# A macaron block on one core: the sums of two of eight batches in the second scoring pass made by accumulating transfers

## The reference

```
x = x + 0.5 * routed_ffn(layernorm(x))     # first pass of the router
x = x + attention(layernorm(x))
x = x + 0.5 * routed_ffn(layernorm(x))     # second pass of the router
```

## Time and profile before

| | us |
|---|---|
| median of 3 runs | 4295.17 (4293.64 to 4295.38) |
| the profiled execution itself | 4294.03 |
| its span in the profile | 4292.0 |
| second scoring pass, first issue of SP to first instruction of the token choice | 3816.65 to 3932.39 |

### The profile page before, as it was taken

The page is one execution under the profiler, slowest core; times in us unless marked ns, Lnnn a source line. Parts: engine busy times, 40 slices in busy tenths (PEclk is TensorE's granted clock), DMA queues, the critical chain, the costliest instruction groups (busy, mean ns, idle before and its releaser), DMA issues. The chain is left out here.

```text
span 4292.0 us, 59690 instructions
## 1 busy us (share of the span) xinstructions
PE 3592.8 (84%) x20178; PEld 1422.3 (33%) x20178; DVE 3187.8 (74%) x4122; ACT 3242.9 (76%) x6717; POOL 2988.4 (70%) x1166
## 2 busy tenths in 40 slices
PE   0376784699999999999999999999999999930376
PEld 0243452233333333333333333333333333310243
DVE  8644674888888888888888888888888888628544
ACT  3544673589988898998898899899889989834433
POOL 2011001399999999999999999999999989975211
PEclk9988897799999999999999999999999999965598
DMA  6500899589999999999999999999999999888300
GB/s 210 168 5 3 296 391 313 118 180 194 210 198 204 206 199 205 198 212 198 204 207 197 207 196 209 202 202 208 198 207 200 206 202 195 170 214 277 124 5 5
DMA packets 335683, 809.46 MB, mean 189 GB/s; under 512 B 27596, under 2 KB 211424, under 8 KB 271648
## 3 DMA queue, kind: packets, MB, share of 16 engines
q0 software_dynamic: 66432, 475.04, 54.9%
q1 hardware_dynamic: 223008, 284.46, 22.7%
q10 hardware_dynamic: 45952, 46.27, 3.1%
HBM read 198.90 MB, written 136.48 MB: 78 GB/s over the span
## 5 line engine op out<-in xcount | busy, mean ns | idle before, releaser
L1703 ACT ACTIVATE at_probs<-at_ps_s 128x512 f32<-128x512 f32 x4096 | 2261.9, 615 | 256.4 <-PE at_ps_s L1813 248.9
L1562 POOL TENSOR_TENSOR at_pool_sum<-at_pool_sum,at_probs 128x2048 f32<-128x2048 f32 x448 | 2173.6, 4852 | 27.8 <-DMA at_probs<-at_probs 20.0
L1592 DVE TENSOR_REDUCE at_part_max<-at_ps_max 128x3 f32<-128x1536 f32 x1024 | 1801.0, 1759 | 428.6 <-PE at_ps_max L1736 428.3
L1813 PE MATMUL at_ps_s<-at_qs,at_ks 97*128 97x512 f32 (+1 forms) x4096 | 1524.4, 451 | 6.4 <-ACT at_probs L1703 5.1
L1782 PE MATMUL at_ps_acc<-at_probs,at_v 128*32 128x512 f32 x8192 | 1092.7, 605 | 0.9 <-ACT at_probs L1703 0.9
L1813 PEld LDWEIGHTS at_ps_s<-at_qs,at_ks 97*128 97x128 f32 (+1 forms) x4096 | 626.5, 188 | 1103.5 <-ACT at_probs L1703 815.5
L1594 DVE TENSOR_REDUCE at_part_max<-at_max_copy 128x1 f32<-128x512 f32 x1024 | 691.7, 675 | 0.0
L1655 ACT COPY at_max_copy<-at_ps_max 128x512 f32<-128x512 f32 x1024 | 610.0, 596 | 102.2 <-PE at_ps_max L1736 102.0
L1541 POOL DMA_DIRECT2D at_probs<-at_probs x448 | 399.7, 892 | 288.4 <-ACT at_probs L1703 240.1
L1736 PE MATMUL at_ps_max<-at_ks,at_qs 32*128 32x512 f32 x4096 | 525.5, 500 | 83.0 <-DMA at_ks<-qk_parts 49.3
L1736 PEld LDWEIGHTS at_ps_max<-at_ks,at_qs 32*128 32x128 f32 x4096 | 197.8, 183 | 442.2 <-issue 393.4
(11 more groups left out here) (196 smaller groups left out, 2405.0 us busy)
## 6 DMA issues: line engine op xcount, KB each, us to landing
at_probs<-at_probs POOLq DMA_DIRECT2D x448, 1024.0 KB, 8.3
qk_parts<-pr_hi SPq DMA_DIRECT2D x32, 1024.0 KB, 12.1
qk_parts<-pr_lo SPq DMA_DIRECT2D x32, 1024.0 KB, 12.3
at_qs<-qk_parts SPq DMA_DIRECT2D x320, 64.0 KB, 5.5
at_ks<-qk_parts SPq DMA_DIRECT2D x80, 256.0 KB, 5.2
rows_tile<-in_x SPq DMA_DIRECT2D x16, 1024.0 KB, 11.9
after_ffn<-rows_tile ACTq DMA_DIRECT2D x16, 1024.0 KB
v_tokens<-pr_v SPq DMA_DIRECT2D x32, 512.0 KB, 10.9
```

The source lines that it names most:

```text
L1562: nc.gpsimd.tensor_tensor(acc, first, probs[:, slot(unit, c)], ALU.add).then_inc(pool_added, 1)
L1592: nc.vector.reduce_max(part_max[:, 0:HG - 1, t, c], ps_max[:, 0:HG - 1], AX.X).then_inc(three_max_done, 1)
L1703: nc.scalar.activation(probs[:, slot(unit, c), h], ps_s[:, BANK[unit, j]], ACT.Exp, scale=SCALE).then_inc(exp_done, 1)
L1813: nc.tensor.matmul(ps_s[:, BANK[unit, j]], ks[rows, g, h, c * P:(c + 1) * P], qs[rows, unit % NQB, h, :], start=True, stop=True).then_inc( ...
```

## The change

Batches 3 and 7 are taken out of the pieces; 24 pieces are left (`PARTS`). For each of the two, SP issues one load of 2 MB of residual rows into `rows.tile` (L177 of the changed kernel) behind the last piece of the batch three before, and GpSimd, once that has landed and after the last piece of the batch two before is added, issues one accumulating transfer of 2 MB (L220) that reads `attention` from memory and adds it onto the held rows. VectorE and the products of GpSimd in these two batches wait for that transfer's semaphore (`dma_summed`) in place of `added`. The products keep their tiles and their number, 32; those of a batch made by transfer follow in one row. Nothing else in the program is changed.

```
+    DMA_BATCHES = (3, 7) if adding else ()
+    PARTS = [(b, p) for b in range(B) if b not in DMA_BATCHES for p in range(PIECES)]
...
+                b, p = PARTS[n]
+                first = b * S + p * PIECE * P
+                tiles = slice(p * PIECE, (p + 1) * PIECE)
                 if n >= NADD:
 
                     sp.wait_ge(added, n - NADD + 1)
...
-                for n in range(1, B * PIECES):
+                for n in range(1, len(PARTS)):
                     load_both(n)
+                    for b in DMA_BATCHES:
+                        if PARTS[n] == (b - 3, PIECES - 1):
+                            sp.dma_start(rows.tile[:, b], x[b * S:(b + 1) * S, :].rearrange("(t p) d -> p t d", p=P)
+                                         ).then_inc(dma_x_in[b], 16)
...
-                if adding:
-                    pool.wait_ge(added, n + 1)
+                if b in DMA_BATCHES:
+                    pool.wait_ge(dma_summed[b], 16)
+                elif adding:
+                    pool.wait_ge(added, PARTS.index((b, n % PIECES)) + 1)
...
-                    if n >= 1:
-                        product(n - 1)
-                product(B * PIECES - 1)
+                    while done < b * PIECES + p:
+                        product(done)
+                        done += 1
+                    if p == PIECES - 1 and b + 2 in DMA_BATCHES:
+                        pool.wait_ge(dma_x_in[b + 2], 16)
+                        nc.gpsimd.dma_start(rows.tile[:, b + 2], add[(b + 2) * S:(b + 3) * S, :]
+                                            .rearrange("(t p) d -> p t d", p=P), accum_op=ALU.add
+                                            ).then_inc(dma_summed[b + 2], 16)
+                while done < SHARED:
+                    product(done)
+                    done += 1
...
-                    if adding and t % PIECE == 0:
-                        dve.wait_ge(added, b * PIECES + t // PIECE + 1)
+                    if b in DMA_BATCHES and t == 0:
+                        dve.wait_ge(dma_summed[b], 16)
+                    elif b not in DMA_BATCHES and adding and t % PIECE == 0:
+                        dve.wait_ge(added, PARTS.index((b, t // PIECE)) + 1)
```

More of the change, by code:

```diff
@@ L123, in score_rows @@
         added = sem("added")
+        dma_x_in = {b: sem(f"dma_x_in{b}") for b in DMA_BATCHES}
+        dma_summed = {b: sem(f"dma_summed{b}") for b in DMA_BATCHES}
         own_done = sem("own")
@@ L150, in load_both @@
                 k = n % NADD
-                first = n * PIECE * P
-                tiles = slice(n % PIECES * PIECE, (n % PIECES + 1) * PIECE)
+                b, p = PARTS[n]
+                first = b * S + p * PIECE * P
+                tiles = slice(p * PIECE, (p + 1) * PIECE)
                 if n >= NADD:
                     sp.wait_ge(added, n - NADD + 1)
-                sp.dma_start(rows.tile[:, n // PIECES, tiles],
+                sp.dma_start(rows.tile[:, b, tiles],
                              x[first:first + PIECE * P, :].rearrange("(t p) d -> p t d", p=P)).then_inc(both_in[k], 16)
@@ L194, in _ @@
             if adding:
-                for n in range(B * PIECES):
-                    tiles = slice(n % PIECES * PIECE, (n % PIECES + 1) * PIECE)
+                done = 0
+                for n, (b, p) in enumerate(PARTS):
+                    tiles = slice(p * PIECE, (p + 1) * PIECE)
                     pool.wait_ge(both_in[n % NADD], n // NADD * 32 + 32)
-                    nc.gpsimd.tensor_tensor(rows.tile[:, n // PIECES, tiles], rows.tile[:, n // PIECES, tiles],
+                    nc.gpsimd.tensor_tensor(rows.tile[:, b, tiles], rows.tile[:, b, tiles],
                                             addend[:, n % NADD], ALU.add).then_inc(added, 1)
```

## The result

The changed kernel takes 4306.87 us (median of 8 runs, 4304.01 to 4312.37), the kernel before 4294.74 (8 runs, 4290.31 to 4298.59): a ratio of 1.003, 95% interval 1.0019 to 1.0041, or 8 to 18 us more. It is slower. The other half is no merit or fault of the forecast: the median grew by 12.1 us, 3 less than the pass of the profiled execution did, which is within the scatter of the stages around it.

The account below looks back on a forecast made before the run. The DMA engines at 348 GB/s were taken as the bound. Last landing 3926.8 plus 2.3 + 2.4 + 9.7 gives 3941.2 against 3922.95, +18.2; 4294.03 + 18.2 = 4312.2, forecast 4313 against the median, range 4299 to 4327 us.

Parts of the forecast that it names:

- The bound: Second scoring pass: the DMA engines set the pace, 348 GB/s for 1 KB rows; GpSimd's relief is worth little.
- the estimate by the Trainium skill's 425 GB/s: Second scoring pass: with loads at 425 GB/s, DMA engines' sum 90 us and the change about 6 us faster; not adopted.
- The cost of a transfer: Each 2.10 MB accumulating transfer: 81 ns per 1 KB run and engine, 10.4 us, against 47 ns and 6.0 us plain.
- The sum's +8.8 us: DMA engines over the second scoring pass: 84.3 us of loads plus 20.8 of transfers, 105.1 against 96.3.
- The 2 MB loads: Residual rows of batches 3 and 7: each load holds up the next piece by 6.0 us, together 12.0 us.
- The issue: GpSimd issuing a transfer of 2048 runs: under 8 us taken, where it costs nothing.
- A long issue: Rival: GpSimd stands still 13.9 us at the second transfer's issue; +21.8 us, 4317; chance 0.14.
- What lands last: End of the pass: loads land after the second transfer, at 3926.8, then 2.3 + 2.4 + 9.7 us; +18.2.
- this case too, +13.6: End of the pass, transfer landing last instead of the loads: batch 7 starts at 3926.8, ends at 3936.5.
- The end: VectorE takes all 16 tiles of batch 7, 9.7 us, only after the last landing and batch 6's last piece.
- Cheap accumulation: Rival: transfers at 47 ns a run, 6.0 us each; +9.4, or +4.8 with the transfer last; chance 0.14.
- dear: Rival: accumulating transfers at 130 ns a run, 16.6 us each; +30.6 us, 4326; chance 0.08.

Follow-up runs that it names:

- e1: Kernel before, but GpSimd adds only the first of each piece's four tiles, three quarters of the sums left out: 4293.28 us, pass 113.6 us.
- e5: Kernel before with rows placed so that loads and stores of held rows are runs of 4 KB, not 1 KB; all sums on GpSimd: 4292.06 us, pass 113.5.
- e2: Changed kernel with only batch 3 summed by an accumulating transfer, the other seven by GpSimd: 4300.15 us, pass 122.6 us.
- e3: Changed kernel with only batch 7 summed by an accumulating transfer: 4304.71 us, pass 125.7 us.
- e6: Changed kernel, batches 3 and 7 by accumulating transfer, with rows placed in runs of 4 KB: 4295.91 us, pass 115.8 us.
- e7: Changed kernel with rows in runs of 4 KB and only batch 3 by accumulating transfer: 4293.40 us, pass 114.9 us.
- e9: Changed kernel with rows in runs of 4 KB and only batch 6 by accumulating transfer, issued a batch earlier: 4292.13 us, pass 116.6 us.

## Why the prediction was right, and where not

- **The bound.** Right. 348 GB/s for rows of 1 KB is the loads' own limit: shorter adds do not raise it (e1), longer runs do (e5). GpSimd and the DMA engines had the same pace to 0.02 us a piece, and relieving one of them gave back 2.2 us at most (e1, e5). On the estimate by the Trainium skill's 425 GB/s, from "DMA: Bandwidth & Descriptors", section "Measured (HBM→SBUF, 128 partitions, SWDGE, issued from GpSimd)": the trace of this kernel disagrees (348), and at 4 KB a run (404 to 410 GB/s, e5) it comes near. The same page of the Trainium skill, section "Where 436 GB/s comes from", gives about 358 GB/s as the limit of the memory for one core, half of what a stack has; e5, with one core at work, is above it.
- **The cost of a transfer.** The term was 81 ns a run; measured were 92 beside loads and 82 alone. The sum's +8.8 us for the DMA engines measured +10.9. Of the 2.1 us between, the runs with one transfer show 0.5 for the first (e2: +4.9 where the sum has 4.4) and 1.4 for the second (e3: +5.8), whose end is uneven. At 92 ns a run the first alone would have cost 5.8, so part of its price came back elsewhere in the phase; where isn't shown.
- **The 2 MB loads.** Right: 6.02 us of GpSimd after the fourth add. After the sixteenth I expected 6 and saw 4.15: the four products of batch 3, which the forecast had not placed there, had put GpSimd behind its loads (five products in a row, 3.46 us from 3881.84).
- **The times in the middle.** The pass began 2.42 us later than before; less that, the twentieth add came at 3905.0 (3904.4 forecast) and the second issue at 3908.0 (3907.4).
- **The issue.** Right that it hides: 1.24 us held, 2.1 recorded. "A long issue" falls. The Trainium skill's sentence on many descriptors ("DMA: Bandwidth & Descriptors", section "Anatomy of one DMA") fits what GpSimd pays: 2048 runs cost 2.1 us recorded, against 0.87 for 128.
- **What lands last.** This step failed. It let the transfer start "a microsecond after the issue", so that the loads followed it at 3926.8, with 2.3 + 2.4 + 9.7 behind. The first packet came 5.8 us after the issue, so the loads got ahead, and the transfer landed last. An estimate from the trace: from the first packet to the loads' last one, 9.0 us at 139 ns, 65 runs of loads went out on each engine; 4.8 us more of loads alone, at 47 ns, are 101. With a start after 1 us these 166 would have stood beside the transfer's 128, and the loads would have come last as forecast. As it was, VectorE started on batch 7 at 3931.20, less 2.42 that is 3928.8, and worked 9.4 us. The prediction named this case too, +13.6; it was +15.2, since the landing was 2.0 us later than 3926.8 and the tiles 0.3 shorter. The +18.2 was 3 us too much. The microsecond had no row behind it, and the trace of the kernel before had some: the attention's accumulating transfers of 128 runs, where GpSimd's queue was empty at the issue, sent their first packet 1.43 to 1.56 us after it when the other queues kept the DMA engines under a tenth busy (33 of them), and 1.44 to 3.16 us when these kept them over 80% busy (19).
- **The end.** Right in kind: a batch that becomes ready at once puts 9.4 us of VectorE behind the last landing, where before one add and one piece stood there, 4.7. The experiments with plain copies and with quarters show it from both sides.
- **The rivals.** Cheap accumulation (+4.8 to +9.4) and dear (+30.6) both fall with 82 to 92 ns. But the plain copies show that even free accumulation cost +9.6, as the upper of the two numbers said.

Left open: why the first packet comes so late. From issue to first packet record it was 5.8 to 5.9 us for 2048 accumulating runs of 1 KB (changed kernel, e2, e3), 4.9 to 5.1 for the plain copies and for quarters of 512 runs, 3.7 to 4.5 for 512 runs of 4 KB (e6, e7, e9), against 1.4 to 3.6 us for the 90 transfers of the attention, 128 runs of 8 KB each, that were issued to an empty GpSimd queue. Two of these runs change one thing alone: a quarter of the runs in an issue makes it 0.8 us less, a plain copy in place of an accumulating one 0.8 to 0.9 less. Neither explains the most of it, and what the loads already queued cause is not shown.

## What to carry to other kernels

When an engine without a gap has the same pace as the DMA engines, look for a stretch of the program that uses one of them alone; it tells which one is the bound, and taking work from the other to the bound makes the kernel slower. An engine that is starved once and has no slack doesn't catch up (e2, e7, e9), so a 2 MB load ahead of 1 MB pieces costs even where the sums agree. And a transfer that completes as one makes everything behind it start at once: what the consumer has to do for it stands on the path, at the end of a stage in full.

## What the hardware showed that I had not expected

- An accumulating run of 1 KB from memory cost 82 ns alone and 92 beside loads, a plain one 47: nearly double, and per byte about what the attention's transfers from on-chip to on-chip memory, in runs of 8 KB, had cost (201.6 GB/s against 200).
- 3.7 to 5.9 us from the issue of a GpSimd transfer to its first packet while SyncE's queue was full, and 1.43 to 1.56 in the attention where the other queues were quiet. The Trainium skill, "DMA: Bandwidth & Descriptors", section "Specifications", gives a first-byte latency of about 1 us for this path; the quiet case comes near it, the pass does not.
- The run length moved loads from 348 to 404 and 410 GB/s, 1 KB against 4 KB, the bytes, the queue and the size of a load being the same.
